# One fused attention and expert layer on one core: another order of loads, weight splits and first tiles at the start

## The chip, the core and the metric

The kernel runs on one NeuronCore of a Trainium2 chip. The metric is the device time of one execution in microseconds (us), as the median of three runs. PE is TensorE, DVE is VectorE, ACT is ScalarE, POOL is GpSimd and SP is SyncE, which here only issues DMAs.

## What is computed

The input x is 4 batches of 512 tokens with 512 values, in float32. Cut to what matters:

```
xn  = layernorm(x)
out = x + attention(xn) + ffn(xn)
ffn(xn) = shared(xn) + sum over 3 chosen of 7 experts of w_e * expert_e(xn)
shared(xn) = (silu(xn @ Ws1) * (xn @ Wsg)) @ Ws2          # all matrices 512 x 512
gate: softmax(xn @ gate_w + gate_b), the best 3 by biased value, renormalised
attention: latent attention, 16 heads of 128 (+64 rotary), causal, 4 x 512 tokens
```

## The kernel before, in words

The 2048 tokens are NT = 16 tiles of P = 128 rows. The change is in the first stage: layernorm of all tiles, their transposes, the shared expert for tiles 0 to 15, and the gate's logits. After it come the latent projections, the routed experts (54 blocks of 128 sorted rows), and attention, none of which is edited beyond names of semaphores. The five engines run five programs written out by hand; each engine takes its instructions in that order, and semaphores hold one back until another engine has come far enough. So the order in each of the five lists, not a planner, sets what waits for what.

Each product in float32 is made of three products in a rounded format: every operand is split in a high half (a rounded copy) and a low half (the original less the high half). A 128-row tile times a 512 x 512 matrix has four chunks of 128 rows of the matrix and so 4 x 3 = 12 matmuls of 512 columns (`rows_by`, whose matmuls are issued in the helper `product`, L48).

The steps of a tile t, with the names used in the text:

- its rows are loaded by a DMA, from ACT's queue (tiles 0 to 7) or SP's (tiles 8 to 15);
- `statistics` on DVE, for two tiles g = t // 2 at a time: BN_STATS (L886) for each, BN_AGGR (L889) for each, and the variance plus epsilon (L891);
- `rstd_of(g)` on POOL (L462), and `shift_of(g)` on DVE (L899);
- `normalise(t)` on ACT (L620), in place;
- `turn_rows(t)` on PE (L1370): four transposes into one of two banks, so tile t waits until tile t - 2 has left its bank;
- `turn_high(t)` on ACT (L625) and `turn_low(t)` on DVE (L905) split the transposed tile and free the bank.

A chunk k of the shared weights (0 to 3 Ws1, 4 to 7 Wsg, 8 to 11 Ws2) is loaded into one of four staging places by SP, rounded by ACT (`split_high`, L615), and its low half is made by POOL (`shared_low`, L467). Chunk k + 4 is loaded into the place of chunk k once the low half of k is made.

PE's list is: transposes of tiles 0 to 3, then for each tile b: `up(b)` (12 matmuls, waits for the low halves of chunks 0 to 3), `turn_hidden(b-1)`, transposes of two more tiles, `gated(b)` (12, chunks 4 to 7), transposes of two more, `logits` of four tiles (8 matmuls of 512 columns), `down(b-1)` (12, chunks 8 to 11). Between them ACT makes `silu(b)` (L645) and `hid_high` (L651), and DVE `multiply(b)` (L927) and `hid_low` (L932). The dictionary TURNS says after which product which tiles are transposed:

```
FIRST_TURNS = 4
TURNS = {0: ((4, 5), (6, 7)), 1: ((8, 9), (10, 11)), 2: ((12, 13), (14, 15))}
```

ACT and DVE have the same loop over b, with `normalise` and `statistics` of later tiles placed between.

## Time and profile before

| what | us |
|---|---|
| median of 3 runs | 1336.71 (1335.64 to 1336.96) |
| the profiled execution | 1336.61 |
| its span, first to last instruction | 1334.8 |
| PE busy in the span | 1305.5 (98%) |
| DVE busy | 738.4 (55%) |
| ACT busy | 620.6 (46%) |
| POOL busy | 629.7 (47%) |

The profiled execution's own time is 1.8 us over its span, which is what lies around the first and the last instruction. A time in the trace counts from the span's start. In a row of a timeline the first number is the start, the second the length of the group, and the bracket tells how long the engine had been idle and which instruction released it. Where a group has several instructions (x8), they overlap a little, so that the group is shorter than their sum. "PEclk" is the share of full speed that TensorE's clock was granted.

### The profile page before, as it was taken

To read this page: it belongs to the slowest core of one execution; us is meant where nothing else is said; L and a number is where in the kernel's file an instruction comes from. 1 tells how busy PE (TensorE), PEld (TensorE's weight loads), DVE (VectorE), ACT (ScalarE), POOL (GpSimd) and SP (SyncE) were. 2 spreads that over 40 slices of the span, in tenths; PEclk is the share of its full clock that TensorE was granted. 3 is DMA by queue.
4 is the path that set the end of the run, shared out by engine and by line. 5 is a ranking of instruction groups with operands and counts; after the bars stand their busy time and mean duration, and the time that the engine had idled before them with its cause. 6 is when DMAs were issued, how large, how long until landed. Compare 5 with 4: busy or idle time off the path is not lost.

```text
span 1334.8 us, 21124 instructions
## 1 busy us (share of the span) xinstructions
PE 1305.5 (98%) x6553; PEld 1091.0 (82%) x6553; DVE 738.4 (55%) x1349; ACT 620.6 (46%) x1146; POOL 629.7 (47%) x534
## 2 busy tenths in 40 slices
PE   5999999999999999999997999999999999999999
PEld 3788898888888888888885888888888888888887
DVE  6361154232222222222225878888888888888876
ACT  6421243222222222222225766676667666756664
POOL 5125584994060006000003467766776677666543
PEclk9999999999999999999998999999999999999999
DMA  8225553664251214312114223233233332322012
GB/s 269 64 88 216 193 185 98 189 182 138 64 145 63 63 52 126 92 51 64 62 42 158 62 50 71 62 64 78 40 78 63 65 65 54 77 42 60 17 48 95
DMA packets 72952, 123.23 MB, mean 92 GB/s; under 512 B 10960, under 2 KB 19280, under 8 KB 72848
## 3 DMA queue, kind: packets, MB, share of 16 engines
q1 hardware_dynamic: 42000, 60.49, 15.8%
q0 software_dynamic: 11312, 27.23, 9.4%
q10 hardware_dynamic: 19536, 34.17, 7.8%
q8 instruction: 60, 0.98, 0.3%
q14 instruction: 44, 0.36, 0.1%
HBM read 74.41 MB, written 39.05 MB: 85 GB/s over the span
## 4 chain that ended last, share of the span: by engine, by line
PE 94%; DVE 2%; issue 1%; POOL 1%; DMA 1%; ACT 1%; ACTq 0%; SPq 0%; DVEq 0%; POOLq 0%
PE bank L48 84%; PE bank L1653 4%; PE bank L1442 2%; PE bank L1384 2%; PE bank L1562 1%; DMA rows_b<-in_x 1%; DVE store_b L1270 0%; PE bank L1370 0%; DVE p_store L1283 0%; POOL slots L467 0%; DVE stats L886 0%; PE bank L1503 0%; DVE acc L1297 0%; DVE store_b L1263 0%; DMA rot_sin<-sum_b 0%
## 5 line engine op out<-in xcount | busy, mean ns | idle before, releaser
L48 PE MATMUL bank<-store_b,store_a 128*128 128x512 f32 (+1 forms) x1536 | 326.2, 365 | 6.3 <-DVE store_b L1270 3.3
L48 PE MATMUL bank<-slots,x_turned 128*128 x1296 | 317.5, 394 | 0.3 <-DVE x_turned L910 0.3
L48 PEld LDWEIGHTS bank<-store_b,store_a 128*128 128x128 f32 x1536 | 256.6, 191 | 60.1 <-issue 8.7
L48 PEld LDWEIGHTS bank<-slots,x_turned 128*128 128x128 f32 x1296 | 239.3, 188 | 48.0 <-issue 0.5
L932 DVE TENSOR_TENSOR hid_t<-bank,hid_t 128x512 fp32r<-128x512 f32 x70 | 48.4, 691 | 342.8 <-ACT hid_t L651 342.8
L48 PE MATMUL bank<-slots,hid_t 128*128 (+1 forms) x840 | 208.5, 397 | 1.7 <-DVE hid_t L932 1.7
L48 PEld LDWEIGHTS bank<-slots,hid_t 128*128 128x128 f32 x840 | 153.7, 188 | 32.7 <-issue 2.0
L48 PE MATMUL bank<-store_b 128*128 128x512 f32 x768 | 179.4, 389 | 0.0
L48 PEld LDWEIGHTS bank<-store_b 128*128 128x128 f32 x768 | 144.1, 188 | 29.9
L825 ACT ACTIVATE p_store<-bank 128x512 f32<-128x512 f32 x160 | 95.6, 598 | 87.0 <-PE bank L48 85.4
L521 POOL CAST slots<-staging 128x512 f32 (+1 forms) x84 | 51.7, 615 | 171.1 <-PE bank L48 169.4
L1270 DVE TENSOR_TENSOR store_b<-p_store,store_b 128x512 fp32r<-128x512 f32 x128 | 125.1, 979 | 0.5 <-ACT store_b L820 0.4
L575 POOL TENSOR_TENSOR store_b<-p_store,store_b 128x512 fp32r<-128x512 f32 x32 | 41.7, 1304 | 171.7 <-ACT store_b L820 171.7
L523 POOL TENSOR_TENSOR slots<-staging,slots 128x512 f32 (+1 forms) x84 | 108.5, 1291 | 14.1 <-POOL slots L521 13.2
L645 ACT ACTIVATE hidden<-bank 128x512 f32<-128x512 f32 x70 | 41.9, 598 | 141.6 <-PE bank L48 135.1
L1283 DVE SCALAR_TENSOR_TENSOR p_store<-p_store,cap 128x512 f32<-128x512 f32 x96 | 93.7, 976 | 21.0 <-ACT p_store L825 20.7
L820 ACT ACTIVATE store_b<-p_store 128x512 fp32r<-128x512 f32 x160 | 100.5, 628 | 2.5 <-DVE p_store L1283 1.9
L48 PE MATMUL bank<-slots,store_a 128*128 128x512 f32 x384 | 96.4, 401 | 3.0 <-POOL slots L467 3.0
L927 DVE TENSOR_TENSOR hidden<-bank,hidden 128x512 f32<-128x512 f32 x70 | 48.4, 691 | 92.1 <-PE bank L48 92.1
L633 ACT ACTIVATE x_turned<-bank 128x512 fp32r<-128x512 f32 x54 | 32.4, 600 | 132.0 <-PE bank L1384 132.0
L663 ACT ACTIVATE y_store<-bank,row_scale 128x512 f32<-128x512 f32 x54 | 37.3, 691 | 121.1 <-PE bank L48 121.1
L1297 DVE SCALAR_TENSOR_TENSOR acc<-bank,inv_store,acc 128x512 f32<-128x512 f32 x128 | 89.3, 737 | 3.2 <-PE bank L48 3.2
(203 smaller groups left out, 1821.2 us busy)
## 6 DMA issues: line engine op xcount, KB each, us to landing
staging<-in_w SPq DMA_DIRECT2D x56, 256.0 KB, 2.7
sorted_y<-y_store ACTq DMA_DIRECT2D x54, 256.0 KB
rows<-sorted_x ACTq DMA_DIRECT2D x51, 260.0 KB, 2.7
rot_sin<-sum_b SPq DMA_DIRECT2D x128, 64.0 KB, 2.0
staging<-in_wg SPq DMA_DIRECT2D x28, 256.0 KB, 2.8
shared_y<-y_store ACTq DMA_DIRECT2D x16, 256.0 KB
raw<-in_wot SPq DMA_DIRECT2D x16, 256.0 KB, 2.8
acc<-in_x SPq DMA_DIRECT2D x16, 256.0 KB, 5.7
```

Of the source, the lines that this page charges most:

```text
L48: made = pe.matmul(out, a, b, start=first and n == 0, stop=last and n == len(pairs) - 1, skip_group_check=onto)
L521: pool.tensor_copy(hi, staged[:, n % NS, :]).then_inc(on["job_high"], 1)
L523: pool.tensor_tensor(lo, staged[:, n % NS, :], hi.bitcast(F32), ALU.subtract).then_inc(on["job_low"], 1)
L645: act.activation(hidden[:, b % 2, :], banks[0], ACT.Silu).then_inc(on["silu_done"], 1)
L820: act.activation(p_hi[g], prob(u, g), ACT.Copy).then_inc(on["p_high"], 1)
L825: act.activation(prob(u, g), ring.bank("scores", u, g), ACT.Exp, scale=SCALE).then_inc(on["exps_done"], 1)
L927: dve.tensor_tensor(hidden[:, b % 2, :], banks[1], hidden[:, b % 2, :], ALU.mult).then_inc(on["mult_done"], 1)
L932: dve.tensor_tensor(hid_t[:, b % 2, 1], banks[2].rearrange("p (c t) -> p c t", c=HC), hid_t[:, b % 2, 0].bitcast(F32), ALU.subtract).then_ ...
L1270: dve.tensor_tensor(p_lo[g], prob(u, g), p_hi[g].bitcast(F32), ALU.subtract).then_inc(on["p_low"], 1)
L1283: made = dve.scalar_tensor_tensor(part, part, low, cap[:, 0:n].unsqueeze(1).broadcast_to([P, BANK // n, n]), ALU.max, ALU.min)
L1297: dve.scalar_tensor_tensor(acc[:, t, :], ring.bank("output", u, tt), inv_store[:, u % 2, tt // 2, 1, tt % 2:tt % 2 + 1], acc[:, t, :], ALU ...
L1653: made = pe.matmul(ring.bank("sums", u)[:, n:n + 1], w, one[:, 0:1], start=True, stop=True)
```

## The change

The reads of tiles 0 and 2 are issued by ACT and those of 1 and 3 by SP, ahead of the weights; chunks are loaded in pairs, one DMA of 512 KB each, tiles 4 and 5 behind chunk 7, the others behind chunk 11. Every one of the 12 chunks has a place of its own (`staged`, `early`, `shared_rest`; the last two lie where later buffers do), so no load waits. POOL rounds chunks 0 to 3 (`first_high`), DVE makes the low halves of chunks 1 and 3 (`first_low`), and POOL makes the other ten. `up` and `gated` of tile 0 run the eight matmuls that need no low half of the weights first, and the four others last. PE starts with 20 transposes of the identity. Tiles 4 to 7 are transposed together after `gated(0)` and `logits(0)`. The lists of ACT, DVE and POOL are reordered. Cut to its core:

```diff
--- before.py
+++ after.py
@@ -169,7 +169,11 @@
         slot0 = slots[:, 0:SLOT].rearrange("p (s k n) -> p s k n", s=2, k=CH)
         staging = tile(experts, "staging", [P, NS * D])
         staged = staging[:].rearrange("p (n d) -> p n d", n=NS)
+        with ExitStack() as ctx:
+            early = tile(ctx, "early", [P, HC, D])
         hid_t = tile(experts, "hid_t", [P, 2, 2, HC, P], F32R)
+        with ExitStack() as ctx:
+            shared_rest = tile(ctx, "shared_rest", [P, CH - NS - HC, D])
         with ExitStack() as ctx:
             cat_raw = tile(ctx, "cat_raw", [P, DC, WC])
         x_turned = [tile(experts, f"x_turned{n}", [P, 2, DC, P], F32R) for n in range(2)]
...
+        def shared_raw(k, n=1):
+
+
+            for place, first, count in ((staged, 0, NS), (early, NS, HC), (shared_rest, NS + HC, CH - NS - HC)):
+                if first <= k < first + count:
+                    return place[:, k - first:k - first + n, :]
...
+        WARM = 20
+        TURNS = {0: ((), (4, 5, 6, 7)), 1: ((8, 9), (10, 11)), 2: ((12, 13), (14, 15))}
         PREFIX = 5
...
             return p_store[:, (NG * u + g) % (NG + 1), :]
 
         def sync_program(sp):
-            def load_shared(k):
+            def load_shared(k, sem):
                 src, lines = chunk_of(k, (ws1, wsg, ws2))
-                staging_free(sp, k)
-                sp.dma_start(staged[:, k % NS, :], src[lines, :]).then_inc(on[f"staged{k % NS}"], 16)
+                src = src[lines.start:lines.start + 2 * P, :].rearrange("(c p) n -> p c n", p=P)
+                sp.dma_start(shared_raw(k, 2), src).then_inc(on[sem], 16)
 
             def load_x(t):
                 sp.dma_start(row_of(t)[:, 0:D], x_t[:, t, :]).then_inc(on[f"x_in{t}"], 16)
 
-            for k in range(NS):
-                load_shared(k)
-            for k in range(NS, CH):
-                load_x(k + NT - CH)
-                load_shared(k)
+            load_x(1)
+            load_x(3)
+            load_shared(2, "first_in1")
+            load_shared(4, "gate_weights_in")
+            load_shared(6, "gate_weights_in")
+            load_x(4)
+            load_x(5)
+            load_shared(8, "down_weights_in")
+            load_shared(10, "down_weights_in")
+            for t in range(6, NT):
+                load_x(t)
             sp.wait_ge(on["zero_made"], 1)
             for n in range(NE):
                 sp.dma_start(sorted_x[(NR - NE + 1 + n) * P:(NR - NE + 2 + n) * P, :], rows_a[:, NA, :]).then_inc(
                     on["zeros_in"], 16)
+            sp.wait_ge(on["shared_low"], CH - 2)
...
+
+            def first_high(k):
+                pool.wait_ge(on[f"first_in{k // 2}"], 16)
+                pool.tensor_copy(slot1[:, 0, k, :], shared_raw(k)).then_inc(on["first_high"], 1)
+
+            def shared_low(k):
+                if k < DC:
+                    pool.wait_ge(on["first_high"], k + 1)
+                else:
+                    pool.wait_ge(on["split_high"], k - DC + 1)
+                pool.tensor_tensor(slot1[:, 1, k, :], shared_raw(k), slot1[:, 0, k, :].bitcast(F32),
+                                   ALU.subtract).then_inc(on["shared_low"], 1)
 
             def rstd_of(g):
                 cols = slice(2 * g, 2 * g + 2)
...
             rstd_of(0)
+            first_high(0)
+            first_high(1)
             rstd_of(1)
+            first_high(2)
+            first_high(3)
             shared_low(0)
-            shared_low(1)
+            shared_low(2)
+            shared_low(4)
             rstd_of(2)
-            shared_low(2)
-            shared_low(3)
+            shared_low(5)
             rstd_of(3)
+            shared_low(6)
+            shared_low(7)
             for g in range(4, NT // 2):
-                shared_low(2 * g - 4)
-                shared_low(2 * g - 3)
+                shared_low(g + 4)
                 rstd_of(g)
             pool.memset(picked[:].bitcast(F32), 0.0).then_inc(on["cleared"], 1)
...
@@ -598,8 +629,10 @@
                     gather(2 * n + 1, j)
 
         def scalar_program(act):
-            for t in range(NT - CH + NS):
+            for t in (0, 2):
                 act.dma_start(row_of(t)[:, 0:D], x_t[:, t, :]).then_inc(on[f"x_in{t}"], 16)
+            act.dma_start(shared_raw(0, 2), ws1[0:2 * P, :].rearrange("(c p) n -> p c n", p=P)).then_inc(
...
-                act.activation(slot[:, 0, n % CH, :], staged[:, n % NS, :], ACT.Copy).then_inc(on["split_high"], 1)
+            def split_high(k):
+                act.wait_ge(on["gate_weights_in" if k < 2 * DC else "down_weights_in"], 32)
+                act.activation(slot1[:, 0, k, :], shared_raw(k), ACT.Copy).then_inc(on["split_high"], 1)
 
             def normalise(t):
                 act.wait_ge(on["shift_made"], t // 2 + 1)
...
                     copy_logits(3)
                 if b == 0:
-                    split_high(8, slot1)
-                    split_high(9, slot1)
-                if b < 2:
-                    for t in range(8 + 4 * b, 10 + 4 * b):
-                        normalise(t)
-                for t in end:
+                    split_high(8)
+                    split_high(9)
+                    copy_logits(0)
+                    turn_high(4)
+                    turn_high(5)
+                    normalise(8)
+                    normalise(9)
+                    turn_high(6)
+                    turn_high(7)
+                    split_high(10)
+                    split_high(11)
+                    normalise(10)
+                    normalise(11)
+                if b == 1:
+                    normalise(12)
+                    normalise(13)
+                for t in end if b else ():
                     turn_high(t)
-                if b < 2:
-                    for t in range(10 + 4 * b, 12 + 4 * b):
-                        normalise(t)
-                if b == 0:
-                    split_high(10, slot1)
-                    split_high(11, slot1)
-                if b <= 2:
+                if b == 1:
+                    normalise(14)
+                    normalise(15)
+                if b in (1, 2):
                     copy_logits(b)
                 if b == 3:
...
                                          ALU.mult).then_inc(on["shift_made"], 1)
+
+            def statistics(g):
+                stats_of(2 * g)
+                stats_of(2 * g + 1)
+                deviations(g)
+
+            def first_low(k):
+                dve.wait_ge(on["first_high"], k + 1)
+                dve.tensor_tensor(slot1[:, 1, k, :], shared_raw(k), slot1[:, 0, k, :].bitcast(F32),
+                                  ALU.subtract).then_inc(on["first_low"], 1)
 
             def turn_low(t):
...
@@ -1198,9 +1248,6 @@
                     hid_low(b - 1)
                 for t in mid:
                     turn_low(t)
-                if b == 0:
-                    statistics(5)
-                    shift_of(5)
                 if b == 1:
                     statistics(7)
                     shift_of(7)
@@ -1208,9 +1255,15 @@
                     for _ in range({4: 3, 5: 10, 6: 5}[b]):
                         next(gate, None)
                 multiply(b)
+                if b == 0:
+                    statistics(4)
                 for t in end:
                     turn_low(t)
+                    if t == 5:
+                        shift_of(4)
                 if b == 0:
+                    statistics(5)
+                    shift_of(5)
                     statistics(6)
                     shift_of(6)
                 if b == 3:
...
+            def rows_by_high(bank, turned, b, m):
+
+                for c in range(DC):
+                    w_hi, w_lo = weights(b, m * DC + c)
+                    product(pe, bank, [(turned[0][:, c, :], w_hi), (turned[1][:, c, :], w_hi)], first=c == 0, last=False)
+
+            def rows_by_low(bank, turned, b, m):
+                return product(pe, bank, [(turned[0][:, c, :], weights(b, m * DC + c)[1]) for c in range(DC)],
+                               first=False)
+
+            def first_up():
+
+                pe.wait_ge(on["turn_low"], 1)
+                pe.wait_ge(on["first_high"], DC)
+                rows_by_high(banks[0], tokens(0), 0, 0)
+                turn_rows(2)
+                turn_rows(3)
+                pe.wait_ge(on["first_low"], 2)
+                pe.wait_ge(on["shared_low"], 2)
+                rows_by_low(banks[0], tokens(0), 0, 0).then_inc(on["up_done"], 1)
+
+            def first_gated():
+                pe.wait_ge(on["split_high"], DC)
+                rows_by_high(banks[1], tokens(0), 0, 1)
+                pe.wait_ge(on["shared_low"], 2 + DC)
+                rows_by_low(banks[1], tokens(0), 0, 1).then_inc(on["gated"], 1)
+
             def rows_by(bank, turned, b, m):
                 hi, lo = turned
...
 
-            for t in range(FIRST_TURNS):
+            pe.wait_ge(on["ident_made"], 2)
+            for _ in range(WARM):
+                pe.transpose(banks[3][:, 0:P], ident[:], ident[:])
+            turn_rows(0)
+            turn_rows(1)
+            first_up()
+            first_gated()
+            logits(0)
+            for t in TURNS[0][1]:
```

**PE, from the start to `down(0)`.** `bank<-ident` is the 20 transposes of the identity; `rows_a`, `rows_b` are tiles' transposes (x8 is two tiles); `slots,store_a` is `up` or `gated`; `store_a,gw` is `logits`; `ident,hidden` is `turn_hidden`. Before:

```order
L1370 MATMUL bank<-ident,rows_a 128x128 x8
L1370 MATMUL bank<-ident,rows_b 128x128 x8
L48 MATMUL bank<-slots,store_a 128x512 x12
L1370 MATMUL bank<-ident,rows_b 128x128 x8
L48 MATMUL bank<-slots,store_a 128x512 x12
L1370 MATMUL bank<-ident,rows_b 128x128 x8
L48 MATMUL bank<-store_a,gw 16x512 x4
L48 MATMUL bank<-store_a,gw 8x512 x4
L48 MATMUL bank<-slots,store_a 128x512 x12
L1442 MATMUL bank<-ident,hidden 128x128 x4
L1370 MATMUL bank<-ident,rows_b 128x128 x8
L1466 MATMUL bank<-ident,lt_store 128x16 x4
```

And in the changed kernel:

```order
L1598 MATMUL bank<-ident 128x128 x20
L1423 MATMUL bank<-ident,rows_a 128x128 x8
L48 MATMUL bank<-slots,store_a 128x512 x8
L1423 MATMUL bank<-ident,rows_b 128x128 x8
L48 MATMUL bank<-slots,store_a 128x512 x16
L48 MATMUL bank<-store_a,gw 16x512 x4
L48 MATMUL bank<-store_a,gw 8x512 x4
L1423 MATMUL bank<-ident,rows_b 128x128 x16
L48 MATMUL bank<-slots,store_a 128x512 x12
L1516 MATMUL bank<-ident,hidden 128x128 x4
L1423 MATMUL bank<-ident,rows_b 128x128 x8
L1540 MATMUL bank<-ident,lt_store 128x16 x4
```

Tiles 2 and 3 now stand inside `up(0)`, the whole of `gated(0)` and `logits(0)` are ahead of tiles 4 to 7, and behind `up(1)` the order is as before.

**DVE, from a `shift_of` to `turn_low(8)` and `(9)`.** `shift<-mv,rstd` is `shift_of`, `stats` and `mv` and `var_eps` are `statistics`, `store_a<-bank` is `turn_low`, `hidden` is `multiply`, `hid_t` is `hid_low`. Before:

```order
L899 SCALAR_TENSOR_TENSOR shift<-mv,rstd 128x2
L927 TENSOR_TENSOR hidden<-bank,hidden 128x512
L905 TENSOR_TENSOR store_a<-bank,store_a 128x4x128 x2
L886 BN_STATS stats<-rows_b 128x6 x2
L889 BN_AGGR mv<-stats 128x2 x2
L891 TENSOR_SCALAR var_eps<-mv 128x2
L899 SCALAR_TENSOR_TENSOR shift<-mv,rstd 128x2
L932 TENSOR_TENSOR hid_t<-bank,hid_t 128x512
L905 TENSOR_TENSOR store_a<-bank,store_a 128x4x128 x2
```

These rows begin with `shift_of(5)`; those of g = 3 and 4 stand ahead of them. In the changed kernel, from `shift_of(4)`:

```order
L937 SCALAR_TENSOR_TENSOR shift<-mv,rstd 128x2
L953 TENSOR_TENSOR store_a<-bank,store_a 128x4x128 x2
L920 BN_STATS stats<-rows_b 128x6 x2
L925 BN_AGGR mv<-stats 128x2 x2
L928 TENSOR_SCALAR var_eps<-mv 128x2
L937 SCALAR_TENSOR_TENSOR shift<-mv,rstd 128x2
L920 BN_STATS stats<-rows_b 128x6 x2
L925 BN_AGGR mv<-stats 128x2 x2
L928 TENSOR_SCALAR var_eps<-mv 128x2
L937 SCALAR_TENSOR_TENSOR shift<-mv,rstd 128x2
L980 TENSOR_TENSOR hid_t<-bank,hid_t 128x512
L953 TENSOR_TENSOR store_a<-bank,store_a 128x4x128 x2
```

Between the multiply of tile 0 and `turn_low(8)` there stood one pair of tiles' statistics before (g = 6); now g = 4 (ahead of these rows), 5 and 6 stand there.

**ACT, from the copy of `logits(0)` to the halves of tiles 8 and 9.** `lt_store` is the copy of the logits, `store_a<-bank` is `turn_high`, `rows_b` is `normalise`, `slots` is `split_high`, `hidden` is `silu(1)`, `hid_t` is `hid_high(0)`. Before:

```order
L620 ACTIVATE rows_b<-rows_b,shift,rstd 128x512 x2
L615 ACTIVATE slots<-staging 128x512 x2
L673 ACTIVATE lt_store<-bank 16x512
L645 ACTIVATE hidden<-bank 128x512
L651 ACTIVATE hid_t<-bank 128x512
L625 ACTIVATE store_a<-bank 128x4x128 x2
```

And in the changed kernel:

```order
L706 ACTIVATE lt_store<-bank 16x512
L658 ACTIVATE store_a<-bank 128x4x128 x2
L653 ACTIVATE rows_b<-rows_b,shift,rstd 128x512 x2
L658 ACTIVATE store_a<-bank 128x4x128 x2
L648 ACTIVATE slots<-shared_rest 128x512 x2
L653 ACTIVATE rows_b<-rows_b,shift,rstd 128x512 x2
L678 ACTIVATE hidden<-bank 128x512
L684 ACTIVATE hid_t<-bank 128x512
L658 ACTIVATE store_a<-bank 128x4x128 x2
```

Ahead of `silu(1)` there now stand four `turn_high`, `normalise` of tiles 8 to 11 and two splits behind the copy of the logits; before, they stood ahead of it.

## Rows read from the trace of the kernel before

**Rows 1.** Busy time by stretch; last columns: PEclk, DMA share, GB/s.
```profile
core 0: us, PE busy (x) PEld busy (x) DVE busy (x) ACT busy (x) POOL busy (x), PEclk, DMA share, GB/s
0.00:45.00 45.00, 28.65 (x134) 22.09 (x135) 28.68 (x64) 28.47 (x50) 22.63 (x33) 1.00 0.73 234
60.00:700.00 640.00, 639.31 (x3155) 533.63 (x3154) 195.07 (x519) 171.42 (x341) 212.75 (x229) 1.00 0.35 110
```
**Rows 2.** Timeline of PE: start us, length us, instructions, [idle before].
```profile
11.87 1.97 PE L1370 MATMUL bank<-ident,rows_a 128*128 128x128 f32 x8 [11.87 <-ACT rows_a L620]
...
19.17 5.07 PE L48 MATMUL bank<-slots,store_a 128*128 128x512 f32 x12 [1.92 <-POOL slots L467]
...
26.23 3.02 PE L48 MATMUL bank<-slots,store_a 128*128 128x512 f32 x12 [1.12 <-POOL slots L467]
...
29.88 2.09 PE L48 MATMUL bank<-store_a,gw 128*16 128x512 f32 x8
31.81 2.91 PE L48 MATMUL bank<-slots,store_a 128*128 128x512 f32 x12
...
39.16 1.03 PE L1370 MATMUL bank<-ident,rows_b 128*128 128x128 f32 x8
...
44.65 2.88 PE L48 MATMUL bank<-slots,store_a 128*128 128x512 f32 x12
```
**Rows 3.** Timeline, first tile: when x rows land, `shift`, and the first `normalise`.
```profile
5.51 0.69 DVE L886 BATCH_NORM_STATS2 stats<-rows_a 128x6 f32<-128x512 f32 x1 [5.51 <-DMA rows_a<-in_x]
...
6.82 0.69 DVE L886 BATCH_NORM_STATS2 stats<-rows_a 128x6 f32<-128x512 f32 x1 [0.61 <-DMA rows_a<-in_x]
...
10.81 0.16 DVE L899 SCALAR_TENSOR_TENSOR shift<-mv,rstd 128x2 f32<-128x2 f32 x1
...
11.00 1.52 ACT L620 ACTIVATE rows_a<-rows_a,shift,rstd 128x512 f32<-128x512 f32 x2 [4.30 <-DVE shift L899]
```
**Rows 4.** Busy time by stretch while both load queues are full.
```profile
5.00:8.00 3.00, 0.00 (x0) 0.00 (x0) 1.80 (x5) 1.50 (x2) 0.00 (x0) 1.00 1.04 398
```
**Rows 5.** Costliest groups: a cast of one weight chunk on GpSimd.
```profile
L521 POOL CAST slots<-staging 128x512 f32 (+1 forms) x84 | 51.7, 615 | 171.1 <-PE bank L48 169.4
```
**Rows 6.** Timeline of ACT, DVE and POOL in tile 1's stretch.
```profile
32.11 1.14 ACT L615 ACTIVATE slots<-staging 128x512 fp32r<-128x512 f32 x2
...
33.94 0.69 POOL L462 TENSOR_TENSOR rstd<-var_eps,neg_half 128x2 f32<-128x2 f32 x1 [2.31 <-DVE var_eps L891]
...
34.59 2.52 POOL L467 TENSOR_TENSOR slots<-staging,slots 128x512 fp32r<-128x512 f32 x2
34.66 1.22 DVE L899 SCALAR_TENSOR_TENSOR shift<-mv,rstd 128x2 f32<-128x2 f32 x1 [0.80 <-POOL rstd L462]
34.75 0.60 ACT L645 ACTIVATE hidden<-bank 128x512 f32<-128x512 f32 x1 [1.04 <-PE bank L48]
...
35.25 0.59 ACT L651 ACTIVATE hid_t<-bank 128x512 fp32r<-128x512 f32 x1
35.72 1.10 ACT L625 ACTIVATE store_a<-bank 128x512 fp32r<-128x512 f32 x2
35.87 0.69 DVE L932 TENSOR_TENSOR hid_t<-bank,hid_t 128x512 fp32r<-128x512 f32 x1
...
36.48 1.28 DVE L905 TENSOR_TENSOR store_a<-bank,store_a 128x512 fp32r<-128x512 f32 x2
36.68 1.54 ACT L620 ACTIVATE rows_b<-rows_b,shift,rstd 128x512 f32<-128x512 f32 x2
37.67 1.27 DVE L886 BATCH_NORM_STATS2 stats<-rows_b 128x6 f32<-128x512 f32 x2
...
38.98 0.25 DVE L889 BATCH_NORM_AGGREGATE mv<-stats 128x2 f32<-128x6 f32 x2
...
39.27 0.17 DVE L891 TENSOR_SCALAR var_eps<-mv 128x2 f32<-128x2 f32 x1
```
**Rows 7.** PE at the start of attention: a row with its wait; then PEclk 0.55.
```profile
728.04 1.32 PE L48 MATMUL bank<-store_b,store_a 128*128 128x256 f32 x6 [2.57 <-DVE store_b L1270]
...
730.00:732.00 2.00, 2.00 (x6) 1.26 (x6) 0.92 (x1) 0.00 (x0) 2.00 (x2) 0.55 0.00 0
```

More of the change, by code:

```diff
@@ L716, in scalar_program @@
             normalise(3)
[L717 to L718 removed]
+            split_high(4)
+            split_high(5)
             turn_high(2)
             turn_high(3)
[L721 to L728 removed]
+            split_high(6)
+            split_high(7)
+            for t in range(4, 8):
+                normalise(t)
             act.wait_ge(on["gate_in"], 48)
@@ L1172, in vector_program @@
             statistics(0)
-            statistics(1)
+            stats_of(2)
             shift_of(0)
-            statistics(2)
+            stats_of(3)
+            deviations(1)
             shift_of(1)
             turn_low(0)
+            first_low(1)
             turn_low(1)
+            first_low(3)
+            statistics(2)
+            turn_low(2)
+            turn_low(3)
             shift_of(2)
             statistics(3)
-            turn_low(2)
-            turn_low(3)
             shift_of(3)
-            statistics(4)
-            shift_of(4)
             dve.wait_ge(on["gw_high"], 1)
```

84 lines of the change are left out of this document (31 added, 53 removed).

## The prediction

> **What bounds the kernel now.** First the stretches [rows 1]: from 60 to 700 us PE is busy 639.31 of 640 us, while from 0 to 45 us it is busy 28.65 of 45. So past the start nothing but PE's own list counts, and a microsecond that PE loses or gains at the start is found again at the end; that rests on the same row, since the other engines there have 171 to 224 us of work in 640. Then PE's timeline of the start [rows 2]. Before 29.88 us it stands idle three times over: until 11.87, 1.92 us before `up(0)` at 19.17, 1.12 us before `gated(0)` at 26.23. It is also slow: 12 matmuls take 5.07 us in `up(0)` and 3.02 in `gated(0)`, so most of `up(0)` ran at the lower of TensorE's two clocks (1.2 GHz, not 2.4). I take the rates as 0.43 and 0.23 us for a matmul of 512 columns ((5.07 - 3.02) / 9 = 0.23 more for each of some nine slow ones), and 0.21 and 0.11 for a transpose. From 29.88 on PE runs without a gap: `up(1)` starts at 31.81, the transposes of tiles 10 and 11 at 39.16, `up(2)` at 44.65. These three points are my milestones. Behind `up(1)` PE's order is unchanged, so `up(2)` in the changed kernel against 44.65 is the whole effect.
>
> **Part 1, the loads: earlier by 2.7 us.** Before, the first two tiles land at 5.51 and 6.82 from one queue, but `shift` of the first pair stands on DVE behind the statistics of the second and starts at 10.81; `normalise(0)` starts at 11.00 [rows 3]. Now tiles 0 and 1 stand first in two queues and land at about 5.5, tiles 2 and 3 at 6.8. Two statistics (1.27), two aggregates (0.25), the variance (0.17), `rstd` on POOL (0.69) [rows 6] and the gaps between give `shift` at 8.2 and `normalise(0)` at 8.35: 2.65 us earlier. Together the queues move 398 GB/s [rows 4], so 0.26 MB takes 0.66 us. Chunks 0 to 3 (1 MB) land 2.6 us after 6.8, at 9.4; chunks 4 to 7, alone on SP's queue by then, at 12.3; tiles 4 to 7 at 13.0 to 17.6.
>
> **Part 2, `up(0)` in two pieces: earlier by 6.5 us, at the slow clock.** POOL rounds chunks 0 and 1 from 9.4, makes `rstd(1)`, rounds 2 and 3: 4 x 0.61 [rows 5] + 0.7 = 12.6. PE transposes tiles 0 and 1 from 9.2 and starts `up(0)` at 12.7, where it stood at 19.17. The 20 transposes of the identity take 20 x 0.21 = 4.3 us and end near 6; then PE is idle for 3 us, transposes two tiles, and is idle for 2 us. An idle stretch of that sort costs the clock in this trace: at the start of attention PE waits 2.57 us and is granted 0.55 in 730 to 732 [rows 7]. So I price eight matmuls at 0.43 (3.6 us, to 16.3), tiles 2 and 3, and the last four: `up(0)` ends near 18.4.
>
> **Part 3, `gated(0)`: the gain is lost on POOL.** Its first eight matmuls need chunks 4 to 7 rounded. ACT's list has normalise 2 and 3 (`shift_of(1)` ends near 12.0), splits 4 and 5, `turn_high` 2 and 3 (PE's transposes end at 17.1), splits 6 and 7: 18.2 + 1.14 = 19.4. They run to 21.4. The last four need the low halves of chunks 6 and 7, and those stand on POOL behind `rstd(3)`, which needs the statistics of tiles 6 and 7, which stand on DVE behind `turn_low(3)` (19.0). From there: 1.27 + 0.25 + 0.17 of statistics, `rstd` 0.69, two low halves 2.52 [rows 6] = 4.9, and 0.2 of gaps: 24.1. PE waits 2.7 us. Then four matmuls (slow) and `logits(0)` run to 28.3. Tiles 4 and 5 follow; tile 6 needs the bank of tile 4, so it waits for the copy of the logits, `turn_high(4)` and `turn_low(4)`, 1.8 us after the logits, to 30.3; tiles 6 and 7 take 1.0. `up(1)` starts at **31.3**, against 31.81: of 6.5 us, 0.5 is left.
>
> **Part 4, the chain ahead of tiles 10 and 11.** This decides. From `up(1)` to the transposes of tile 10 PE has 39.16 - 31.81 = 7.35 us of work [rows 2], and is there at 38.6. Tile 10 needs tile 8's bank, so `turn_low(8)`, and DVE has the statistics of four tiles ahead of it:
>
> - ACT ends `turn_high(7)` at 33.4: `turn_high` 4 and 5, normalise 8 and 9 (1.54), then 6 and 7. `turn_low(7)` ends at 34.2.
> - `statistics(5)`: 1.27 + 0.25 + 0.17 and gaps, to 35.95; `rstd(5)` to 36.7.
> - `shift_of(5)` takes 1.22 us, not 0.16: it ends when POOL's low half that began with it ends. In the trace `rstd` ends at 34.63, the low halves start at 34.59, and `shift` runs from 34.66 for 1.22 us [rows 6]; the one at 10.81, with no low half beside it, took 0.16 [rows 3]. In the changed kernel a low half again stands right behind `rstd` on POOL: 38.0.
> - ACT meanwhile: normalise 10 and 11 (to 39.5) stand ahead of `silu(1)` (0.60) and `hid_high(0)` (0.59): 40.5.
> - DVE: `statistics(6)`, `rstd(6)` (40.5), `shift_of(6)` held again (41.75), `hid_low(0)` 0.61, `turn_low(8)` 0.68 [rows 6]: **43.0**.
>
> So PE waits 43.0 - 38.6 = 4.4 us in a place where it had no wait. What is queued behind on PE is all of its list. From there `up(2)` was 44.65 - 39.16 = 5.49 away: 48.5. The idle stretch costs the clock once more; eight transposes at 0.10 more each and some seven of the logits' matmuls at 0.20 more each make 2.2. `up(2)` at **50.7**. Sum: -0.5 + 4.4 + 2.2 = **+6.1 us**. The rest of the first stage has no further wait, for the statistics are all done by 46. Edits at nothing: the loads of Ws2 and of tiles 8 to 15, done by 23 us; the zero rows and the projection weights on SP, which now wait for POOL's tenth low half near 38, and are used in the projections only; one semaphore less.
>
> The profiled execution took 1336.61 us, 0.1 below the median of 1336.71; so 1336.7 + 6.1 = **1342.8 us**.
>
> **Bounds.** A low half on DVE has two operands in SBUF and no row here; nearest are 0.68 (`turn_low`) and 1.22 (`shift` beside a low half); I take 0.68, since it is off the chain by a microsecond. A cast on POOL beside DVE: 0.61 to 1.25 (a low half); at 1.25 `up(0)` is 2.5 us later and the total +9.3. Loads later by 2 us: +7.6. Clock: at most 2.2 + 1.6 us less.
>
> VectorE and GpSimd hold each other up by a lock on a shared pair of ports: so the Trainium skill, SBUF — State Buffer, section Who interferes with whom; whichever starts first keeps it for its whole instruction. By that rule the trace agrees, with 1.22 against 0.16 us for the same `shift`.
>
> **Rivals.**
>
> - **The 20 transposes warm PE, and it stays warm** (0.10). The mechanism: full rate at 6 us, kept through waits of 2 to 4 us. Then `up(0)` ends sooner, `gated(0)` is still held to 23.4, `up(1)` starts at 29.2, tile 10 at 41.2, and `up(2)` at 41.2 + 5.5 = 46.8: +2.3, **1339.0**. Against it: rows 7. The Trainium skill, TensorE: Matmul & The Clock Gate, section Part 1: The HAM clock gate (the "warmup" mystery), says that sustained work brings the full clock, which is this rival; the slow `up(0)` after idle stretches of 1.44 and 1.92 us speaks for the other side.
> - **`shift` isn't held by POOL** (0.12), because the low half starts later than it: two times 1.1 us less on the chain, less a smaller loss of clock: +3.4, **1340.1**. Against it: the rows of 34.59 and 34.66 differ by 0.07 us and the order on POOL is the same.
> - **Casts or loads are later** (0.10): +7.6 to +9.3, **1345**.
> - **Faster** (0.05): the chain of part 4 is over when PE gets there. It decides from the point where `turn_low(8)` ends before `gated(1)` does, some 5 us earlier than I have it. Then only the start counts: with no held `shift` and a warm PE `up(1)` starts at 28.1, 3.7 us earlier: **1333.0**. For it: part 1 is nearly certain. Against it: seven statistics, splits and normalisations that lay in idle time of ACT and DVE before 30 us now stand between `logits(0)` and `turn_low(8)`.
> - **The change doesn't do what it says**: the warming may warm nothing. That is in the forecast already.
>
> **How the numbers follow.** The forecast has 0.63: 1342.8, and its own range is +4.4 to +7.4. A measurement of this kernel can tell about 0.2% (2.7 us) from no change. Slower by more than that are the forecast, the held-less `shift` and the late loads, 0.83 when 0.02 of the forecast's lower end is taken off; within it lie the warm PE and that end, 0.12; faster has 0.05. The range reaches down to the lower rivals at 1337.8, and up to the late loads at 1345.2, and leaves out the faster case and the slowest casts.
>
> **What would show it.** Right: `shift` of the first pair at 8.2; eight matmuls of `up(0)` at 12.7, at 0.43 us each; an idle PE of 2 to 3 us inside `gated(0)`, released by POOL; `up(1)` at 31.3; one wait of 4.4 us ahead of the transposes of tiles 10 and 11, released by DVE's `turn_low` (L953); two `shift` of 1.2 us just before; `up(2)` at 50.7. Wrong: no wait ahead of tile 10, or a gap as large later, or a time of attention that differs from before by more than a microsecond.

## The result and the profile after

| | us | runs |
|---|---|---|
| before | 1336.18 (1334.83 to 1338.37) | 6 |
| changed kernel | **1341.32** (1340.39 to 1343.48) | 6 |
| the changed kernel's profiled execution | 1340.39, span 1338.7 | 1 |

The ratio is 1.0043, with a 95% interval of 1.0033 to 1.0053: 5.1 us slower, where 6.1 were forecast (1342.8 us, range 1337.8 to 1345.2). The profiled execution was the shortest of the six; it is 3.8 us above the profiled one of before.

Busy time by stretch in the changed kernel, to be laid beside [rows 1]; PEclk stands third from the end:

```profile
core 0: us, PE busy (x) PEld busy (x) DVE busy (x) ACT busy (x) POOL busy (x), PEclk, DMA share, GB/s
0.00:45.00 45.00, 29.94 (x129) 22.69 (x130) 26.59 (x59) 23.90 (x40) 21.71 (x30) 0.82 0.61 215
60.00:700.00 640.00, 638.95 (x3154) 532.80 (x3153) 194.68 (x519) 171.78 (x341) 213.72 (x229) 1.00 0.35 110
```

The long stretch is as full of PE work as before (638.95 against 639.31 us). In the first 45 us PE is busy longer (29.94 against 28.65 us), and its clock was the low one for part of them. (The 1.00 in rows 1 isn't a measurement: in that trace the first record of the clock comes at 23.65 us. There the slow `up(0)` tells the clock by its duration.)

PE's timeline in the changed kernel, for [rows 2]: start, length, instructions, in brackets how long PE had been idle and who released it.

```profile
1.60 4.16 PE L1598 MATMUL bank<-ident 128*128 128x128 f32 x20 [1.60 <-POOL ident L471]
8.54 1.90 PE L1423 MATMUL bank<-ident,rows_a 128*128 128x128 f32 x8 [2.78 <-ACT rows_a L653]
12.81 3.75 PE L48 MATMUL bank<-slots,store_a 128*128 128x512 f32 x8 [2.36 <-DVE store_a L953]
16.36 1.91 PE L1423 MATMUL bank<-ident,rows_b 128*128 128x128 f32 x8
17.92 1.62 PE L48 MATMUL bank<-slots,store_a 128*128 128x512 f32 x4
19.99 2.11 PE L48 MATMUL bank<-slots,store_a 128*128 128x512 f32 x8 [0.45 <-ACT slots L648]
24.82 1.33 PE L48 MATMUL bank<-slots,store_a 128*128 128x512 f32 x4 [2.72 <-POOL slots L486]
25.95 3.48 PE L48 MATMUL bank<-store_a,gw 128*16 128x512 f32 x8
...
32.38 3.00 PE L48 MATMUL bank<-slots,store_a 128*128 128x512 f32 x12
...
44.02 1.94 PE L1423 MATMUL bank<-ident,rows_b 128*128 128x128 f32 x8 [4.05 <-DVE store_a L953]
45.61 3.76 PE L48 MATMUL bank<-store_a,gw 128*16 128x512 f32 x8
...
52.13 2.88 PE L48 MATMUL bank<-slots,store_a 128*128 128x512 f32 x12
```

`up(0)` starts 6.4 us earlier than before, at the low clock. Then 2.72 us inside `gated(0)` are lost to POOL, `up(1)` starts 0.57 us *later* than before (32.38 against 31.81), and then come 4.05 us of waiting for tile 8's halves. The idle stretch costs the clock: the eight transposes take 1.94 us instead of 1.03 and the logits 3.76 instead of 2.09. `up(2)` is at 52.13 against 44.65: +7.5 us.

The timeline of the other engines, the chain that ends in that wait (for [rows 6]):

```profile
33.98 1.29 DVE L953 TENSOR_TENSOR store_a<-bank,store_a 128x512 fp32r<-128x512 f32 x2 [2.07 <-ACT store_a L658]
35.19 1.27 DVE L920 BATCH_NORM_STATS2 stats<-rows_b 128x6 f32<-128x512 f32 x2
...
37.03 0.69 POOL L493 TENSOR_TENSOR rstd<-var_eps,neg_half 128x2 f32<-128x2 f32 x1 [6.47 <-DVE var_eps L928]
37.68 1.29 POOL L486 TENSOR_TENSOR slots<-shared_rest,slots 128x512 fp32r<-128x512 f32 x1
37.81 1.18 DVE L937 SCALAR_TENSOR_TENSOR shift<-mv,rstd 128x2 f32<-128x2 f32 x1 [0.86 <-POOL rstd L493]
...
39.02 1.52 ACT L653 ACTIVATE rows_b<-rows_b,shift,rstd 128x512 f32<-128x512 f32 x2 [3.55 <-DVE shift L937]
...
41.94 0.74 DVE L937 SCALAR_TENSOR_TENSOR shift<-mv,rstd 128x2 f32<-128x2 f32 x1 [1.27 <-POOL rstd L493]
...
43.20 1.27 DVE L953 TENSOR_TENSOR store_a<-bank,store_a 128x512 fp32r<-128x512 f32 x2
```

POOL had been idle for 6.47 us ahead of `rstd(5)` at 37.03, and then puts a low half right where DVE wants `shift`. Between `turn_low(7)` at 33.98 and `turn_low(8)` at 43.20 DVE does the statistics of tiles 10 to 13, none of which `turn_low(8)` needs.

### The profile page after: what moved, and what is told of

It is laid out like the page before. It is cut to its first block, busy times and chain, and to the rows that moved or that the text cites. A ratio compares the mean times of both kernels' runs of the same rounds, so it can differ in the third digit from the quotient of the medians.

```text
span 1338.7 us, 21148 instructions
## 1 busy us (share of the span) xinstructions
PE 1310.4 (98%) x6573; PEld 1093.9 (82%) x6573; DVE 742.2 (55%) x1351; ACT 619.9 (46%) x1142; POOL 631.0 (47%) x536
## 4 chain that ended last, share of the span: by engine, by line
PE 95%; DVE 2%; issue 1%; POOL 1%; ACT 0%; DMA 0%; ACTq 0%; DVEq 0%; POOLq 0%
PE bank L48 85%; PE bank L1735 4%; PE bank L1516 2%; PE bank L1437 2%; PE bank L1644 1%; POOL slots L486 0%; PE bank L1423 0%; POOL rstd L493 0%; DMA rows_a<-in_x 0%; DVE store_b L1323 0%; DVE p_store L1336 0%; DVE stats L920 0%; PE bank L1577 0%; PE bank L1553 0%; DVE shift L937 0%
```

## The experiments

My theory after this profile: the loss has two places, low halves 6 and 7 behind `rstd(3)` (ahead of `up(1)`) and the statistics ahead of `turn_low(8)` (behind it); the early loads are a gain. The rivals: the waits move elsewhere when one is taken away; the held `shift` carries the loss; the 20 transposes do something after all. Every kernel was timed in turn with the kernel before, which took 1336.14 us (1336.08 beside the second and fourth move together and beside the reordered kernel without the transposes; 1336.18 beside the changed kernel). Ratio means the time as a share of before's, with its 95% interval. The column of `up(2)` comes from one execution of each kernel, and TensorE's clock falls and rises at other moments in each: from tile 10's transposes to `up(2)` the trace has 8.11 us in the changed kernel and 7.22 without the 20 transposes, for the same instructions. So differences of 1 us in that column alone prove nothing; the waits and starts shown below do.

| run | `up(2)` less 44.65, us | time, us | less before, us |
|---|---|---|---|
| changed kernel | +7.5 | 1341.32 | +5.1 |
| no 20 transposes | +6.7 | 1343.37 | +7.2 |
| low halves 6, 7 first | +5.9 | 1340.21 | +4.1 |
| low halves 9 to 11 first | +7.3 | 1340.46 | +4.3 |
| statistics(6) behind `turn_low(9)` | +3.1 | 1338.00 | +1.9 |
| the second and the fourth move | +1.0 | 1336.06 | 0.0 |
| all three moves | -0.6 | 1334.13 | -2.0 |
| before, with early rows | -3.0 | 1333.61 | -2.5 |
| all four lists reordered | (-8.0 at `up(3)`) | **1327.17** | **-9.0** |
| the same without the 20 transposes | (-8.0 at `up(3)`) | 1327.73 | -8.4 |

**Without the warming.**

```diff
-        WARM = 20
+        WARM = 0
```

> The changed kernel without the 20 transposes of the identity. The transposes raised the clock before the real work in the changed kernel, but only for one granted stretch; it is back at the lower level before up(0) starts at 12.8. Theory A (the loss is the chain of waits on DVE, ACT and POOL): no difference that can be measured, up(1) at 32.4, up(2) at 52.1, 0 +- 0.5 us in all. Theory B (the loss or gain hangs on TensorE's clock at the start): without the transposes tiles 0 and 1 and up(0) come later by 0.5 us or more and the end by 1 to 3 us.

1343.37 us (1340.63 to 1343.39), ratio 1.0046 (1.0032 to 1.0060). PE's timeline:

```profile
13.22 3.75 PE L48 MATMUL bank<-slots,store_a 128*128 128x512 f32 x8 [2.72 <-DVE store_a L953]
...
32.52 2.99 PE L48 MATMUL bank<-slots,store_a 128*128 128x512 f32 x12
```

The eight matmuls of `up(0)` take 3.75 us with and without, and `up(1)` is at 32.52 against 32.38. The time is less clean than theory A had it: it asked for 0 +- 0.5 us, and the median is 2.05 us above the changed kernel's, which is in the range of theory B. But the ratios differ by 0.0003 only (0.4 us), their intervals overlap almost wholly, and `up(2)` stands at 51.39, earlier than the 52.13 with the transposes. So no loss at the start is seen, and none in the time that can be told from nothing. The rival of a PE that stays warm has fallen already by the changed kernel's own trace, where `up(0)` ran at the low clock.

**Low halves 6 and 7 ahead of `rstd(3)` on POOL.**

```diff
             shared_low(5)
-            rstd_of(3)
             shared_low(6)
             shared_low(7)
+            rstd_of(3)
```

> The changed kernel with one move on POOL: the low halves of chunks 6 and 7 stand ahead of rstd of tiles 6 and 7. Theory A: the wait of 2.7 us ahead of the last four matmuls of gated(0) goes, they start at 21 instead of 24.8, up(1) at 29.5 to 31; the later chain moves with it, so about 2 to 3 us of it are left at up(2) and at the end. Theory C (POOL is not what holds gated(0); it is the loads of the weights or ACT's splits): no change at gated(0).

1340.21 us (1339.49 to 1342.49), ratio 1.0032 (1.0022 to 1.0041).

```profile
25.09 0.19 DVE L1237 TENSOR_TENSOR gw<-gw_raw,gw 128x32 fp32r<-128x32 f32 x1 [1.70 <-ACT gw L757]
```

```profile
22.39 1.20 PE L48 MATMUL bank<-slots,store_a 128*128 128x512 f32 x4 [0.62 <-POOL slots L486]
25.34 2.02 PE L48 MATMUL bank<-store_a,gw 128*16 128x512 f32 x8 [1.75 <-DVE gw L1237]
...
30.30 3.00 PE L48 MATMUL bank<-slots,store_a 128*128 128x512 f32 x12
...
42.35 1.94 PE L1423 MATMUL bank<-ident,rows_b 128*128 128x128 f32 x8 [4.44 <-DVE store_a L953]
```

The wait inside `gated(0)` falls from 2.72 to 0.62 us, but `logits(0)` now waits 1.75 us for the split gate weights (`gw`), which ACT makes behind `normalise` 6 and 7. That wait is not made by the move: `gw` was split at 25.27 in the changed kernel and is at 25.09 here, and there the longer wait for POOL had hidden it. (`rstd(3)` comes later, but `shift(3)`, with no low half beside it, takes 0.16 instead of 1.15 us and ends at 23.39 instead of 23.56.) PE had the full clock: the logits take 2.02 us, not 3.48. `up(1)` comes 2.1 us earlier. The wait ahead of tile 10 grows from 4.05 to 4.44. So 1.6 us remain at `up(2)`, and some 1 us of time, where theory A had 2 to 3; the intervals of this ratio and the changed kernel's overlap.

**Low halves 9 to 11 ahead of the late `rstd`.**

```diff
-            for g in range(4, NT // 2):
-                shared_low(g + 4)
-                rstd_of(g)
+            shared_low(8)
+            rstd_of(4)
+            shared_low(9)
+            shared_low(10)
+            shared_low(11)
+            rstd_of(5)
+            rstd_of(6)
+            rstd_of(7)
```

> The changed kernel with one move on POOL: the low halves of chunks 10 and 11 stand ahead of rstd of tiles 10 to 15, so that no low half begins beside the shift of tiles 10 to 13. Theory A with the hold: both shifts take 0.16 us instead of 1.18 and 0.74, the transposes of tile 10 start at 42.5 instead of 44.0, up(2) at 49.7 instead of 52.1, and the whole is 1.5 to 2.5 us faster than the changed kernel. Theory E (the shift is slow for a reason of its own, such as waiting for its operands): its length stays and so does the time.

1340.46 us (1338.25 to 1342.78), ratio 1.0030 (1.0017 to 1.0043). DVE and PE:

```profile
38.47 0.79 DVE L933 TENSOR_SCALAR var_eps<-mv 128x2 f32<-128x2 f32 x1
40.12 0.16 DVE L942 SCALAR_TENSOR_TENSOR shift<-mv,rstd 128x2 f32<-128x2 f32 x1 [0.86 <-POOL rstd L493]
...
44.74 1.68 PE L1428 MATMUL bank<-ident,rows_b 128*128 128x128 f32 x8 [3.08 <-DVE store_a L958]
```

With no low half behind `rstd`, `shift` takes 0.16 us: it was the low half that held it. But the low halves now lie beside the variance, which takes 0.79 us instead of 0.17. The wait ahead of tile 10 shrinks by 1.0 us, to 3.08, and `up(1)` to tile 10 takes 10.67 us instead of 11.64. In this execution `logits(0)` and the transposes behind it ran at the low clock (`up(1)` at 34.07, 1.7 us later than in the changed kernel), so that `up(2)`, at 51.90, hides the gain. The run missed its forecast of 49.7 for `up(2)` and of 1.5 to 2.5 us of time; its 0.9 us is inside the interval. The hold is shown; it was worth 1 us of the 7.5, not the loss itself.

**`statistics(6)` and `shift_of(6)` behind `turn_low(9)`; on ACT `normalise` 10 and 11 behind `turn_high(9)`.**

```diff
+                if b == 1:
+                    statistics(6)
+                    shift_of(6)
...
-                    statistics(6)
-                    shift_of(6)
```

> The changed kernel with two moves: on ACT normalise of tiles 10 and 11 stand behind silu(1), hid_high(0) and turn_high of tiles 8 and 9; on DVE the statistics and shift of tiles 12 and 13 stand behind hid_low(0) and turn_low of tiles 8 and 9. Theory A: the wait of 4.05 us ahead of the transposes of tiles 10 and 11 falls to about 0.7 us, that is from a start at 44.0 to one at 40.4, the clock is not lost there, up(2) starts at 47.5 instead of 52.1, and the whole is 4.5 us faster than the changed kernel (about 1336.7). Theory C (transfers, or the weights' splits, set tile 10): the wait stays.

1338.00 us (1335.73 to 1338.84), ratio 1.0011 (1.0001 to 1.0020). PE:

```profile
40.70 1.23 PE L1423 MATMUL bank<-ident,rows_b 128*128 128x128 f32 x8 [0.36 <-DVE store_a L953]
...
44.97 2.98 PE L48 MATMUL bank<-slots,hid_t 128*128 128x512 f32 x12 [1.20 <-POOL slots L486]
```

The wait of 4.05 us falls to 0.36, and the clock stays high (transposes 1.23, not 1.94). A new wait of 1.20 us appears ahead of `down(0)`: low half 11 stands on POOL behind `rstd(6)`, whose statistics I had just moved back. `up(2)` gains 4.3 us, the time 3.3, where 4.6 and 4.5 were forecast. This is the largest single piece.

**The second and the fourth of these moves together, and all three.** The edits are those above.

> The changed kernel with two of the three moves: low halves 6 and 7 ahead of rstd(3) on POOL, and statistics(6)/normalise 10, 11 behind the halves of tiles 8 and 9. up(2) stood 1.6 us earlier with the first move alone, 4.3 us with the second alone, 8.1 us with all three. Theory A (the two savings add, since one lies ahead of up(1) and the other behind it, and the third move brings some 2 us by the split of chunks 8 to 11): up(2) at 46.2 (-5.9), time 1336.0 (1335 to 1337). Theory B (the third move brings nothing here either, and the two together already take all waits away): up(2) at 44.0, as with all three, time 1334.1. Theory C (the second move only hides the first one's saving): up(2) near 47.8, time 1338.

> The changed kernel with the three moves together (low halves of chunks 6 and 7 ahead of rstd of tiles 6 and 7; those of 10 and 11 ahead of rstd of tiles 10 to 15; normalise 10 and 11 behind turn_high 9, and statistics of tiles 12 and 13 behind turn_low 9). Theory A: the waits fall away together: gated(0)'s last four matmuls at 21.5 to 22.5, up(1) at 30, tile 10 at 37.6, up(2) at 43.2 to 44.5; that is level with the kernel before or 1.5 us faster: 1334.5 to 1336.5. Theory B or C (something else makes the loss): it stays 3 us or more above the kernel before.

Two moves: 1336.06 us (1335.49 to 1337.68), ratio 1.0002 (0.9993 to 1.0011). All three: 1334.13 us (1332.16 to 1335.78), ratio 0.9982 (0.9973 to 0.9991). The savings at `up(2)` were 1.6 and 4.3 us singly and are 6.5 together; with the third they are 8.1. So the two places do add, and the third move is worth 1.6 us at `up(2)` and 1.9 us of time here, where it had been worth 1 at most alone. Its place is the wait ahead of `down(0)`, as two moves show it in PE's timeline:

```profile
42.81 2.98 PE L48 MATMUL bank<-slots,hid_t 128*128 128x512 f32 x12 [1.19 <-POOL slots L486]
```

With all three moves that wait is gone (`down(0)` at 41.28).

**The kernel before, with only its rows loaded early** (and the first `shift` ahead of the second pair's statistics, as in the changed kernel).

```diff
+            load_x(1)
+            load_x(3)
             for k in range(NS):
                 load_shared(k)
...
-            for t in range(NT - CH + NS):
+            for t in (0, 2, 4, 5, 6, 7):
...
             statistics(0)
-            statistics(1)
             shift_of(0)
+            statistics(1)
```

> The kernel before with one part of the change alone: the rows of tiles 0 and 2 first on ACT's queue and those of tiles 1 and 3 first on SP's, ahead of the weights, and the shift of tiles 0 and 1 ahead of the statistics of tiles 2 and 3. Theory A: the first transposes start 3.3 us earlier (8.5), up(0) 3 us earlier (16), but gated(0) only 1 us earlier (25.2), since chunks 4 to 7 must wait for the four staging places; up(2) at 44.6 to 45.8, so the end moves by -0.2 to +1.2 us. Theory D (an earlier start is a gain in full): up(2) and the end 2.5 to 3 us earlier.

1333.61 us (1332.07 to 1335.79), ratio 0.9978 (0.9969 to 0.9987): faster than before. PE:

```profile
8.55 1.97 PE L1372 MATMUL bank<-ident,rows_a 128*128 128x128 f32 x8 [8.55 <-ACT rows_a L622]
...
16.21 5.46 PE L48 MATMUL bank<-slots,store_a 128*128 128x512 f32 x12 [1.92 <-POOL slots L469]
...
41.67 2.88 PE L48 MATMUL bank<-slots,store_a 128*128 128x512 f32 x12
```

Theory A was wrong here, and for a plain reason: I had left the loads of chunks 4 to 7 at their old times, though each waits for a low half in the same staging place. The low halves came 3 us earlier, so did the loads, and the 3 us stayed through to `up(2)`. Theory D (the gain in full) had it right. Set against this run, the rest of the change (places of its own for each chunk, splits on POOL and DVE, pieces of `up(0)`, new lists) costs 7.5 + 3.0 = 10.5 us at `up(2)`.

**All four lists reordered.** The loads, places and splits of the changed kernel, with the lists of PE, ACT, DVE and POOL for the first three tiles written as tables. In them `t` is `turn_...`, `n` normalise, `S` statistics (on DVE), `h` shift (DVE) or `turn_hidden` (PE), `r` rstd, `l` shared_low, `u` up, `g` gated, `L` logits, `d` down, `uh`, `ul`, `gh` and `gl` the pieces of `up(0)` and `gated(0)`:

```diff
+        FIRST_POOL = ("r0 r1 f0 f1 f2 f3 l0 l2 l4 r2 l5 l6 l7 r3 l8 l9 r4 l10 l11 r5 r6 r7 ").split()
+        FIRST_DVE = ("S0 s2 s3 h0 d1 h1 t0 t1 f1 t2 f3 S2 h2 t3 S3 gw S4 h3 m0 t4 S5 h4 t5 H0 S6 t6 t7 h5 h6 S7 "
+                     "t8 m1 t9 t10 t11 h7 H1 m2 t12 t13 t14 t15 ").split()
+        FIRST_PE = ("w20 t0 t1 t2 uh t3 ul gh u1 t4 t5 gl L0 h0 g1 t6 t7 d0 t8 t9 L1 b0 t10 t11 u2 t12 L2 h1 g2 "
+                     "t13 d1 b1 t14 t15 ").split()
```

> The changed kernel's loads, places and splits, but with the orders of all four lists up to tile 2 found by playing the measured durations through the semaphores: up(1) runs ahead of gated(0)'s last four matmuls, which wait for POOL, each tile is transposed when its bank is free, and silu and hid_high stand ahead of later tiles' normalisations. Theory A (the loads and splits are good and only the order is bad): up(1) at 17.7, the last four matmuls of gated(0) at 21.3, up(2) at 34.8, up(4) at 58.6 instead of 76.1; the end 9 to 10 us earlier than before, about 1327. If the order is not what costs, it is not faster than 1333.6, which the kernel before with the rows first reaches.

1327.17 us (1326.80 to 1328.33), ratio 0.9934 (0.9920 to 0.9947): 9.0 us faster than before and 14 faster than the changed kernel. PE:

```profile
12.30 3.76 PE L48 MATMUL bank<-slots,store_a 128*128 128x512 f32 x8
...
16.57 5.74 PE L48 MATMUL bank<-slots,store_a 128*128 128x512 f32 x24
...
49.44 2.99 PE L48 MATMUL bank<-slots,store_a 128*128 128x512 f32 x12
```

From 12.30 to 60 us no bracket is left: PE is busy 48.00 of the 48 us from 12 to 60. The 24 matmuls at 16.57 are the rest of `up(0)`, the first eight of `gated(0)` and all of `up(1)`, which fills the time in which POOL makes low halves 6 and 7; `up(3)` is at 49.44, where before has it at 57.46. The time is as forecast (`up(2)` at 36.65, where 34.8 was expected). So with these lists the changed loads and splits are worth 8 to 9 us; the order of the lists had turned that into a loss. What new lists alone would give on the loads of the kernel before wasn't run.

**The same without the 20 transposes.**

> The reordered version (1327.17) without the 20 transposes of the identity; all else the same. Its up(0) starts at 12.30 and its first eight matmuls took 3.76 us, 0.47 each, with the transposes. Theory A (they warm nothing that is still warm at 12 us, as in the changed kernel, where leaving them out changed up(1) by 0.1 us): up(0) again at 12.3 to 12.7 and 3.7 us long, time 1327.2 (1326.5 to 1328). Theory B (they bring the full clock forward to somewhere between 16 and 24 us, so that without them some of the 24 matmuls that follow stay slow): up to 12 matmuls at 0.20 more, time 1328 to 1329.6.

1327.73 us (1326.39 to 1329.60), ratio 0.9935 (0.9922 to 0.9949), with `up(0)` at 12.27 for 3.75 us and `up(3)` at 49.41. Theory A: nothing that can be measured is lost by leaving them out, here either.

## Why the prediction was right

The sign, the three places and the chain of part 4 hold. The closeness of 5.1 to 6.1 is in part luck: `up(2)` came 1.4 us later than forecast, and 2.4 us came back behind it, where the forecast had nothing.

- **Part 1.** `shift` was forecast at 8.2 and came at 7.48, since the rows landed 0.7 us earlier (4.79 for the first statistics):

```profile
4.79 1.29 DVE L920 BATCH_NORM_STATS2 stats<-rows_a 128x6 f32<-128x512 f32 x2 [4.79 <-DMA rows_a<-in_x]
...
7.48 0.16 DVE L937 SCALAR_TENSOR_TENSOR shift<-mv,rstd 128x2 f32<-128x2 f32 x1 [0.32 <-issue]
```

- **Part 2.** `up(0)` was forecast at 12.7, at 0.43 us for a matmul, and started at 12.81, at 0.47. What released it was not POOL's last cast (done at 12.66) but `turn_low(0)` (done at 12.72), held up on DVE behind `shift_of(1)`, whose `rstd(1)` stood on POOL behind the first two casts. The mean granted clock from 9 to 19 us was 0.50. Missed: at that clock the transposes of tiles 2 and 3 take 1.91 us and the last four matmuls 1.62. `up(0)` ended at 19.54, not 18.4. (The count of idle stretches of PE before 29.88 was one short: before, it also stood 1.44 us ahead of tiles 2 and 3, at 15.28.)
- **Part 3.** The last four of `gated(0)` ran at 24.82 (forecast 24.1) after 2.72 us idle (2.7), and `up(1)` started at 32.38, not 31.3. That is +0.6 instead of -0.5 at `up(1)`: the term of the sum that was mis-sized. The slow end of `up(0)` was not the reason. The run with `statistics(6)` moved has the same lists up to here; in it the clock rose at 16.22, `up(0)` ended at 18.27 and `turn_low(3)` at 19.03, as forecast, and yet the last four came at 25.21. What part 3 left out is that `shift_of(2)` stands on DVE between `turn_low(3)` and `statistics(3)`, and POOL's low half of chunk 5 holds it. First the changed kernel, then that run:

```profile
18.55 1.30 POOL L486 TENSOR_TENSOR slots<-early,slots 128x512 fp32r<-128x512 f32 x1
...
19.54 0.33 DVE L937 SCALAR_TENSOR_TENSOR shift<-mv,rstd 128x2 f32<-128x2 f32 x1
19.79 1.27 DVE L920 BATCH_NORM_STATS2 stats<-rows_b 128x6 f32<-128x512 f32 x2
```

```profile
18.57 1.28 POOL L486 TENSOR_TENSOR slots<-early,slots 128x512 fp32r<-128x512 f32 x1
18.95 0.92 DVE L937 SCALAR_TENSOR_TENSOR shift<-mv,rstd 128x2 f32<-128x2 f32 x1
...
20.09 1.36 DVE L920 BATCH_NORM_STATS2 stats<-rows_b 128x6 f32<-128x512 f32 x2 [0.22 <-DMA rows_b<-in_x]
```

In both, `shift` ends at 19.87, with POOL's low half, whenever it began; in the second `statistics(3)` waited for tile 6's rows besides. So 0.7 of the 1.1 us lies ahead of the last four; the other 0.4 is theirs and the logits' (25.95 for 3.48 us, at the low clock), 4.6 us together where 4.2 were forecast.

- **Part 4.** Every link had its size. Tile 10 stood at 44.02 (43.0, the whole difference from part 3), after 4.05 us (4.4), released by `turn_low`. `shift` took 1.18 us where 1.22 was forecast; the second was held for only 0.74. The slow clock cost 52.13 - 44.02 - 5.49 = 2.6 us (2.2). Taking the statistics away from there gave back 4.3 us, and moving the low halves showed the hold by itself.
- **The sum.** `up(2)` was forecast at +6.1 and stood at +7.5; the time was +5.1. The step that failed is that what is lost at the start is found again at the end. It rested on [rows 1], which stop at 700 us, and the forecast's own sign of being wrong, a time of attention that differs by more than a microsecond, came true: in the profiled pair 3.6 of the 7.5 us came back in attention. The same instructions are 7.6 us later at 723.41 (715.80 before), 5.9 later at 762.95 (757.03) and still at 1184.20 (1178.27), and 3.9 later at 1202.78 (1198.90), which is the difference of the spans. In both places before ran at the low clock and the changed kernel did not; that made some 1.6 of the first 1.7 us and 1.5 of the last 2.0, in which before also waited 0.27 us for DVE at 1191.40. First before, then the changed kernel:

```profile
718.34 1.48 PE L48 MATMUL bank<-store_a,wr_store 128*128 128x512 f32 x3
...
1180.00:1200.00 20.00, 19.73 (x96) 0.91 0.24 40
...
1198.90 3.65 PE L48 MATMUL bank<-store_b,store_a 128*128 128x256 f32 x20
```

```profile
725.13 0.84 PE L48 MATMUL bank<-store_a,wr_store 128*128 128x512 f32 x3
...
1180.00:1200.00 20.00, 20.00 (x111) 1.00 0.29 44
...
1202.78 3.65 PE L48 MATMUL bank<-store_b,store_a 128*128 128x256 f32 x20
```

The same three matmuls took 1.48 us before and 0.84 after; from 716.6 to 719.9 and from 1194.5 to 1197.8 us before was granted 0.50. The first was slow (1.48) also with all three moves, and 0.84 in the three changed kernels that were as late as the changed one, but 0.84 also in before with early rows and in the reordered kernel, which were earlier than before; so how late a kernel is doesn't settle it. The second was 1.00 in every kernel with the change's loads and 0.91 in the two with the loads of before or nearly so. Why a stretch 700 or 1100 us later falls at one or the other clock was not tried and stays open. The table shows its size: from `up(2)` (or `up(3)`) to the end the differences move by -3.0 to +0.5 us.

- **The rivals.** "PE stays warm" fell by the changed kernel's `up(0)`, at 0.47 us for a matmul. "`shift` isn't held" fell by the row at 37.81, and by the run that took the hold away. "Casts or loads are later" fell: a cast took 0.59 us. (Its +9.3 doesn't follow from its own terms: an `up(0)` 2.5 us later gives at most 6.1 + 2.5 = 8.6.) "Faster" had its point: the chain over when PE gets there. That didn't come in the changed kernel, but all three moves bring it about, and the time is then below before's.

The clock's behaviour in numbers: full clock was granted from 5.25 to 8.66 us, after the 20 transposes and through 2.78 us in which PE was idle, and then half until 18.9. The Trainium skill, TensorE: Matmul & The Clock Gate, section Part 1: The HAM clock gate (the "warmup" mystery), has the full clock follow sustained work; the trace agrees, with 5.25 us for the first full clock behind work from 1.60 on. It isn't the same in each execution. Of the seven profiled kernels with the 20 transposes, five have a full clock between 5.25 and 10.2 us; in the two others (low halves 6 and 7 first, 9 to 11 first) no full clock is on record before 17.38 us, after the same 20 transposes. In all seven the first eight matmuls of `up(0)` ran at the low one (3.65 to 3.76 us). The early full clock was of no use here, since PE's work didn't go on.

## What to carry to other kernels

When loads or splits come earlier, read on every engine what stands between the freed instruction and the one that TensorE waits for next: here statistics, normalisations and splits that once filled idle time had slid in ahead of `turn_low(8)`. All four lists in another order were worth 14 us on the changed kernel, the early rows alone 2.5 on the one before. Take a wait away together with the one that stands behind it: singly two of these moves gave 1.6 and 4.3 us at `up(2)` and uncovered waits of 1.75 and 1.20; all three gave 8.1. Warming TensorE ahead of gaps of 2.78 and 2.36 us bought nothing here. And a microsecond at the start is a microsecond of time only to within the clock's own comings and goings, here up to 3.
